# Column sums of a low-rank term in a fused FFN kernel: one fp32 selection matmul against two fp32r passes, and its place in the first block of a half

## The chip, the cores and the metric

The kernel runs on one core of one Trainium2 chip. The metric is the device time of one execution in microseconds, as the median of several. The arithmetic is fp32 throughout: TensorE takes fp32 operands either directly or as fp32r pairs (a rounded part and the remainder), which this kernel prepares on ScalarE (the rounded part) and GpSimd or VectorE (the remainder).

## The reference

2048 tokens of width 1024 go through two residual blocks with LayerNorm. The first is a gated FFN (2752 wide) in which the smaller half of each token's gate values is set to zero; the second is a gated FFN whose weights repeat four times and carry low-rank terms of rank 2. The change touches only the low-rank term of the second block's down projection.

```python
x = _layernorm(x + sparse_gated_ffn(x, w_gate, w_up, w_down))

def _qlora_linear(x, wq, A, B):
    w = jnp.tile(wq, (1, 4))
    return x @ w.T + (x @ A.T @ B.T) * 0.5
gate = jax.nn.silu(_qlora_linear(x, w1q, a1, b1))
up   = _qlora_linear(x, w3q, a3, b3)
x = _layernorm(x + _qlora_linear(gate * up, w2q, a2, b2))
```

With h = gate * up (2752 values a token), the down projection needs h folded four times (688 values) against w2q, and the two sums of h against the rows of a2, which are then multiplied by b2.

## The kernel before

The tokens are worked on in NB = 4 blocks of TB = 512, each of NT = 4 tiles of 128 tokens. The first FFN is `gate`, `up` and `down` for blocks 0 to 3 and takes the first 1436 us. The second FFN then runs in two halves h = 0 and 1; half h takes the blocks 2h and 2h + 1. A half is PAIRS = 11 pairs of steps for each of its two blocks (`pair(h, p, bb)`), and then `down_2(2h)` and `down_2(2h + 1)`, the down projections. Each engine has its own instruction stream written out by hand in this order, and the streams meet at semaphores only. Nothing is reordered by a scheduler.

**The sums of h.** In each pair VectorE multiplies gate and up (`h2`), adds them to the folded h (`fold`), and adds h times a column of a2 to `acc[:, bb, r, :]` for r = 0, 1 (four operations of 512 columns, line 1485). `acc` then holds, for 128 partitions, partial sums that still have to be summed over the partitions. After the last pair of a block VectorE raises `acc_ready` (`sums_done`).

**The selection, `low_rank_h(b)` on TensorE.** Two fp32 matmuls with `sel` (128 x 98, all zero but one column with 0.5) as the stationary operand sum `acc` over the partitions into rows 96 and 97 of PSUM bank 4, and raise `t2_done`. ScalarE's `high_t2(b)` (line 957) rounds the two rows into the last chunk of `hqh`; VectorE's `low_rank_h(b)` (line 1500) writes the remainder into `hql` and raises `t2_ready`. The last chunk (c = CQ - 1 = 5, 98 rows) of the down projection then carries the low-rank term with it.

**The down projection, `down_2(b)` on TensorE.** `product(t, n, c)` is three matmuls for token tile t, half n of the columns and chunk c. `all_but_last(t, n)` is the five chunks c = 0 to 4, so 15 matmuls. The results of tile t stand in banks 2(t % 2) + n. The order before is: tile 0 but for its last chunks, `low_rank_h(b)`, in block 0 the twelve transposes `turn_folded(2, k)`, then tile (1, 0) but for its last chunk, then a wait for `t2_ready`, the last chunks of (0, 0), (0, 1) and (1, 0), then (1, 1), and then tiles 2 and 3. Before tile t >= 2 it waits in `bank_waits(t)` until VectorE has taken tile t - 2 out of the same banks (`e_evac`, raised by `take_out`, line 1511).

**VectorE and ScalarE behind the selection.** VectorE's `second(0)` begins with `low_rank_h(0)`; behind it stand, in this order, `low_xf(2, 0)` and `(2, 1)` (line 1419, which wait for ScalarE's `high_xf`), `low_rank_x(2)`, two tiles of `norm_sums`, and only then `take_out(0, 0)`. ScalarE's `second(0)` begins with `high_t2(0)` and goes on to `high_xf(2, 0)` and `(2, 1)` (line 950). In blocks 2 and 3 `take_out` follows `low_rank_h` at once. GpSimd makes the remainders of the folded h (`low_q`, line 734) and of the weights (`low_13`, line 659). Ahead of the second FFN VectorE prepares its constants, `sel` among them (`fill`, line 1375, and line 1391), while GpSimd makes the last remainders of `w_down` and `w2`.

## Time and profile before

| | us |
|---|---|
| median of 3 runs | 1863.69 |
| lowest and highest | 1860.75, 1864.17 |
| profiled execution | 1862.13 |
| its span in the profile | 1860.2 |
| TensorE (PE) busy | 1840.7 |
| DVE, POOL, ACT busy | 1468.3, 957.5, 719.9 |

The profile gives the busy time of each engine, the chain of work that ended last, and the waits by engine and line. PE is TensorE, PEld its weight loads, DVE is VectorE, ACT is ScalarE, POOL is GpSimd. Times in rows are microseconds from the start of the span. A matmul of 512 columns is recorded with 0.39 us while the next one starts 0.23 us after it, so distances between starts are what a stream of matmuls costs.

### The profile page before, as it was taken

How to read it: one execution, taken by the hardware profiler on the slowest of the kernel's cores; microseconds unless marked ns; L12 is line 12 of the kernel's file. 1: busy time of each engine (PE TensorE's matmuls, PEld its weight loads, DVE VectorE, ACT ScalarE, POOL GpSimd, SP SyncE). 2: the span in 40 equal slices, each digit the busy share in tenths (PEclk: the TensorE clock that was granted, in tenths of full speed). 3: DMA queues.
4: the chain of work that ended last, by engine and by line, in shares of the span. 5: the costliest groups of instructions: out<-in, count | busy, mean ns of one | idle time of the engine just before them, and what ended most of it. 6: DMA issues, size and time to landing. Idle time of an engine off the chain costs nothing.

```text
span 1860.2 us, 23661 instructions
## 1 busy us (share of the span) xinstructions
PE 1840.7 (99%) x8584; PEld 1533.3 (82%) x8584; DVE 1468.3 (79%) x2077; ACT 719.9 (39%) x1177; POOL 957.5 (51%) x705
## 2 busy tenths in 40 slices
PE   9999999999999999999999999999999999999998
PEld 8898888978889789888888988888887777777776
DVE  2138899988988695898878768988588899889973
ACT  4346544474233434722343365233323232223312
POOL 5446697546655854465466545554568232023410
PEclk9999999999999999999999999999999999999999
DMA  4333248734377743334786334366953112312212
GB/s 147 93 101 97 86 147 236 204 98 142 97 232 227 226 129 104 113 128 131 236 256 195 93 107 142 98 212 193 278 179 141 35 46 101 135 62 77 102 46 91
DMA packets 123511, 258.65 MB, mean 139 GB/s; under 512 B 13860, under 2 KB 35876, under 8 KB 120168
## 3 DMA queue, kind: packets, MB, share of 16 engines
q1 hardware_dynamic: 118784, 240.34, 41.7%
q10 hardware_dynamic: 4608, 16.78, 2.2%
q8 instruction: 68, 1.11, 0.2%
q14 instruction: 51, 0.42, 0.1%
HBM read 215.65 MB, written 41.42 MB: 138 GB/s over the span
## 4 chain that ended last, share of the span: by engine, by line
PE 83%; POOL 5%; DVE 5%; ACT 4%; DMA 3%; issue 1%; SPq 0%; POOLq 0%; DVEq 0%; ACTq 0%
PE banks L1596 28%; PE banks L1597 27%; PE banks L1598 27%; POOL wl L659 3%; ACT junka L815 2%; DMA w_in_place<-in_wg 2%; DVE junkx L1083 1%; PE banks L1788 1%; POOL xTl L659 1%; ACT wh L766 1%; POOL w2l L659 1%; DMA w_in_place<-in_wd 0%; DVE qa L1125 0%; POOL w L688 0%; PE banks L1801 0%
## 5 line engine op out<-in xcount | busy, mean ns | idle before, releaser
L659 POOL TENSOR_TENSOR wl<-w_in_place,wh 128x512 fp32r<-128x512 f32 (+2 forms) x552 | 751.8, 1367 | 573.1 <-ACT wh L766 571.9
L766 ACT CAST wh<-w_in_place 128x512 fp32r<-128x512 f32 (+2 forms) x560 | 329.0, 589 | 724.2 <-DMA w_in_place<-in_wg 281.2
L1596 PE MATMUL banks<-wh,xTh 128*128 128x512 f32 (+2 forms) x1536 | 565.0, 368 | 5.4 <-POOL wl L659 5.3
L1598 PE MATMUL banks<-wh,xTl 128*128 128x512 f32 (+2 forms) x1536 | 563.2, 367 | 0.0
L1597 PE MATMUL banks<-wl,xTh 128*128 128x512 f32 (+2 forms) x1536 | 563.1, 367 | 0.0
L1596 PEld LDWEIGHTS banks<-wh,xTh 128*128 128x128 f32 x1536 | 288.3, 188 | 51.4 <-POOL wl L659 9.6
L1598 PEld LDWEIGHTS banks<-wh,xTl 128*128 128x128 f32 x1536 | 288.3, 188 | 40.1
L1597 PEld LDWEIGHTS banks<-wl,xTh 128*128 128x128 f32 x1536 | 288.3, 188 | 39.6
L1596 PE MATMUL banks<-wh,hTh 128*128 128x512 f32 x672 | 263.2, 392 | 2.2 <-POOL wl L659 2.1
L1598 PE MATMUL banks<-wh,hTl 128*128 128x512 f32 x672 | 262.2, 390 | 0.0
L1597 PE MATMUL banks<-wl,hTh 128*128 128x512 f32 x672 | 262.2, 390 | 0.0
L815 ACT ACTIVATE junka<-v,negt 128x1376 int8<-128x1376 f32 x96 | 138.3, 1441 | 79.4 <-DVE negt L1093 79.4
L1329 DVE TENSOR_TENSOR hTl<-landed,hTh 128x512 fp32r<-128x512 f32 (+1 forms) x96 | 105.2, 1126 | 73.7 <-ACT hTh L831 73.4
L1596 PEld LDWEIGHTS banks<-wh,hTh 128*128 128x128 f32 x672 | 126.6, 188 | 31.9 <-POOL wl L659 5.5
L1099 DVE TENSOR_SCALAR_CACHE_REDUCE junkd<-v,tc 128x2752 int8<-128x2752 f32 x48 | 147.6, 3076 | 0.9
L1598 PEld LDWEIGHTS banks<-wh,hTl 128*128 128x128 f32 x672 | 126.6, 188 | 26.3
L1597 PEld LDWEIGHTS banks<-wl,hTh 128*128 128x128 f32 x672 | 126.5, 188 | 25.9
L1485 DVE SCALAR_TENSOR_TENSOR acc<-h,a2raw,acc 128x512 f32<-128x512 f32 (+1 forms) x168 | 144.3, 900 | 1.5
L1596 PE MATMUL banks<-xsh,w13h 128*128 128x512 f32 (+1 forms) x352 | 142.5, 405 | 2.4 <-DVE y L1511 1.4
L1597 PE MATMUL banks<-xsl,w13h 128*128 128x512 f32 (+1 forms) x352 | 137.6, 391 | 0.0
L1598 PE MATMUL banks<-xsh,w13l 128*128 128x512 f32 (+1 forms) x352 | 137.3, 390 | 0.0
L659 POOL TENSOR_TENSOR w13l<-w_in_place,w13h 128x512 fp32r<-128x512 f32 x44 | 65.2, 1500 | 88.5 <-ACT w13h L945 88.4
(151 smaller groups left out, 2194.9 us busy)
## 6 DMA issues: line engine op xcount, KB each, us to landing
w_in_place<-in_wd SPq DMA_DIRECT2D x176, 256.0 KB, 2.7
w_in_place<-in_wg SPq DMA_DIRECT2D x128, 256.0 KB, 3.0
w_in_place<-in_wu SPq DMA_DIRECT2D x128, 256.0 KB, 2.7
turning<-squares SPq DMA_DIRECT2D x16, 1024.0 KB, 5.1
landed<-turning SPq DMA_DIRECT2D x64, 256.0 KB, 3.9
w_in_place<-in_w SPq DMA_DIRECT2D x54, 256.0 KB, 2.9
x_in_place<-in_xT SPq DMA_DIRECT2D x32, 256.0 KB, 5.2
y<-in_xtok SPq DMA_DIRECT2D x4, 2048.0 KB, 8.5
```

The lines of the kernel that those rows point to most:

```text
L659: nc.gpsimd.tensor_tensor(lo, landed, hi.bitcast(F32), ALU.subtract).then_inc(done, 1)
L766: nc.scalar.copy(hi, piece).then_inc(hi_done, 1)
L815: ins = nc.scalar.activation(junka[:, :], v[:, t, h * (I // 2):(h + 1) * (I // 2)], ACT.Sign, bias=negt[:, t:t + 1], accum_out=ssum[:, t - ...
L1083: step(V.scalar_tensor_tensor(out=junkx[:, :], in0=x[:, :], scalar=1.0, in1=v[:, R * w + r, I - H:I], op0=ALU.mult, op1=ALU.mult, accum_ou ...
L1099: step(V.tensor_scalar(junkd[:, :], v[:, t, :], tc[:, 0, t:t + 1], None, ALU.is_lt, ALU.add, accum_out=tc[:, 1, t:t + 1]))
L1329: V.tensor_tensor(h_part(hTl, j, g), h_part(landed, j, g), h_part(hTh, j, g).bitcast(F32), ALU.subtract).then_inc(t_lo, 1)
L1485: step(V.scalar_tensor_tensor(out=part, in0=h2[0:rows, i, :], scalar=w, in1=part, op0=ALU.mult, op1=ALU.add))
L1596: nc.tensor.matmul(dst, ah, bh, start=start, stop=False)
L1597: nc.tensor.matmul(dst, ah, bl, start=False, stop=False)
L1598: return nc.tensor.matmul(dst, al, bh, start=False, stop=stop)
L1788: nc.tensor.matmul(banks[4 * (s % 2) + 2 * w + i][0:rows, :], b13[p0:p0 + 3 * R, mm], lx[p0:p0 + 3 * R, bb, :], start=False, stop=True).th ...
```

## The change

The sums `acc` of a block are split like every other operand: ScalarE rounds them into `acch` (`high_sums(b)`, one cast of 128 x 1024, raising `acc_hi`), GpSimd writes the remainder over `acc`, under the name `accl` (`low_sums(b)`, one subtraction of 128 x 1024, raising `acc_lo`), and TensorE sums both over the partitions with `selr`, a copy of `sel` of the type fp32r. There is one `acch` for all blocks, so `high_sums(b)` waits for the selection of block b - 1 (`t2_done`). In the first block of a half (0 and 2) the selection moves from behind tile 0 to behind tile (1, 0), and the last chunks of tiles (0, 0), (0, 1) and (1, 0) move behind the first five of (1, 1). In blocks 1 and 3 the places stay. VectorE has one more copy, from `sel` to `selr`, in its preparation.

```diff
@@ GpSimd
+            def low_sums(b):
+                pool.wait_ge(acc_hi, b + 1)
+                nc.gpsimd.tensor_tensor(accl[:, b % 2, :, :], acc[:, b % 2, :, :], acch[:, :, :].bitcast(F32), ALU.subtract)\
+                    .then_inc(acc_lo, 1)
...
+                low_sums(2 * h)
                 low_q(h, CQ - 1, 1)
+                low_sums(2 * h + 1)
@@ ScalarE
+                high_sums(2 * h)
                 high_q(h, CQ - 1, 1)
+            def high_sums(b):
+                act.wait_ge(acc_ready, b + 1)
+                if b:
+                    act.wait_ge(t2_done, b)
+                nc.scalar.copy(acch[:, :, :], acc[:, b % 2, :, :]).then_inc(acc_hi, 1)
...
                 if b != 1:
                     high_t2(b)
+                if b % 2 == 0:
+                    high_sums(b + 1)
@@ VectorE
             for r in range(R):
-                V.memset(sel[:, r, T2 + r:T2 + r + 1], LORA).then_inc(sel_ready, 1)
+                fill(sel[:, r, T2 + r:T2 + r + 1], LORA)
+            V.tensor_copy(selr[:, :, :], sel[:, :, :]).then_inc(sel_ready, 1)
@@ TensorE
-                pe.wait_ge(acc_ready, b + 1)
+                pe.wait_ge(acc_lo, b + 1)
...
                 for r in range(R):
-                    ins = nc.tensor.matmul(banks[4][0:LR, :], sel[:, r, :], acc[:, b % 2, r, :], start=r == 0, stop=r == R - 1)
+                    nc.tensor.matmul(banks[4][0:LR, :], selr[:, r, :], acch[:, r, :], start=r == 0, stop=False)
+                    ins = nc.tensor.matmul(banks[4][0:LR, :], selr[:, r, :], accl[:, b % 2, r, :], start=False, stop=r == R - 1)
...
-                low_rank_h(b)
+                if b % 2:
+                    low_rank_h(b)
                 if b == 0:
                     for k in range(KQ + 1):
                         turn_folded(2, k)
                 bank_waits(1)
                 all_but_last(1, 0)
+                if b % 2 == 0:
+                    low_rank_h(b)
+                all_but_last(1, 1)
                 pe.wait_ge(ql_done, FOLDS * h + 2 * (CQ - 1) + bb + 1)
                 pe.wait_ge(t2_ready, b + 1)
                 pe.sem_inc(passed_pe, 1)
                 product(0, 0, CQ - 1)
                 product(0, 1, CQ - 1)
                 product(1, 0, CQ - 1)
-                all_but_last(1, 1)
                 product(1, 1, CQ - 1)
```

TensorE's stream in block 0, before: from the last matmul of tile (0, 1) to the first of tile (1, 0). `ident` with `xa` or `rep` are the transposes `turn_folded(2, k)`.

```order
L1598 MATMUL banks<-w2h,hq0l 128x512
L1801 MATMUL banks<-acc,sel 98x512 [waits acc_ready,s_done]
L1801 MATMUL banks<-acc,sel 98x512
L1730 MATMUL banks<-ident,xa 128x128 [waits h_done,xf_in]
L1730 MATMUL banks<-ident,xa 128x128 x3
L1730 MATMUL banks<-ident,xa 128x128 [waits h_done,xf_in]
L1730 MATMUL banks<-ident,xa 128x128 x3
L1730 MATMUL banks<-ident,rep_121 128x128 [waits h_done,rep_ready]
L1730 MATMUL banks<-ident,rep_121 128x128 x3
L1596 MATMUL banks<-w2h,hq0h 128x512 [waits h_done]
```

The same stream after, further on: the end of tile (1, 0) and the start of tile (1, 1).

```order
L1620 MATMUL banks<-w2h,hq0h 128x512
L1621 MATMUL banks<-w2l,hq0h 128x512
L1622 MATMUL banks<-w2h,hq0l 128x512
L1825 MATMUL banks<-acch,selr 98x512 [waits acc_lo,s_done]
L1826 MATMUL banks<-accl,selr 98x512
L1825 MATMUL banks<-acch,selr 98x512
L1826 MATMUL banks<-accl,selr 98x512
L1620 MATMUL banks<-w2h,hq0h 128x512
L1621 MATMUL banks<-w2l,hq0h 128x512
```

The selection now stands behind the twelve transposes and the 15 matmuls of tile (1, 0), has four matmuls for two, and waits for GpSimd in place of VectorE.

ScalarE's stream at the end of half 0, before:

```order
L971 CAST hq0h<-fold_115 96x512 [waits f_done]
L971 CAST hq1h<-fold_116 96x512 [waits f_done]
L957 CAST hq0h<-banks 2x512 [waits t2_done]
L950 CAST xsh<-banks 128x512 [waits xf_turned] x2
L852 ACTIVATE y<-y,nbias,rstd 128x1024 [waits nb_ready]
```

and after:

```order
L984 CAST hq0h<-fold_117 96x512 [waits f_done]
L1021 CAST acch<-acc 128x1024 [waits acc_ready]
L984 CAST hq1h<-fold_118 96x512 [waits f_done]
L970 CAST hq0h<-banks 2x512 [waits t2_done]
L1021 CAST acch<-acc 128x1024 [waits t2_done,acc_ready]
L963 CAST xsh<-banks 128x512 [waits xf_turned] x2
L865 ACTIVATE y<-y,nbias,rstd 128x1024 [waits nb_ready]
```

One cast of the sums stands ahead of the last `hq1h`, and the other between `high_t2(0)` and the two `xsh` casts.

## Rows read from the trace of the kernel before

**Rows 1.** The page: busy time of TensorE, share of the span, instructions.

```profile
PE 1840.7 (99%) x8584; PEld 1533.3 (82%) x8584; DVE 1468.3 (79%) x2077; ACT 719.9 (39%) x1177; POOL 957.5 (51%) x705
```

**Rows 2.** TensorE's waits in the whole run: us in total, times, longest.

```profile
PE banks L1596 <- POOL wl L659: 7.3, 13, 1.8
PE banks L1596 <- DVE y L1511: 1.4, 1, 1.4
```

**Rows 3.** Timeline of TensorE in block 0: start, us, line, operation, [idle before].

```profile
1581.79 1.88 PE L1801 MATMUL banks<-acc,sel 128*98 128x512 f32 x4
1583.51 1.04 PE L1730 MATMUL banks<-ident,xa 128*128 128x128 f32 x8
...
1584.74 0.47 PE L1596 MATMUL banks<-w2h,hq0h 128*128 128x512 f32 x1
...
1588.25 0.40 PE L1596 MATMUL banks<-w2h,hq0h 98*128 98x512 f32 x1
...
1594.44 0.39 PE L1596 MATMUL banks<-w2h,hq0h 128*128 128x512 f32 x1
```

**Rows 4.** Timeline of ScalarE in block 0: the two rows, then the folded x.

```profile
1583.71 0.58 ACT L957 CAST hq0h<-banks 2x512 fp32r<-2x512 f32 x1 [1.83 <-PE banks L1801]
1584.31 1.07 ACT L950 CAST xsh<-banks 128x512 fp32r<-128x512 f32 x2
```

**Rows 5.** Timeline of VectorE in block 0, from the last sums to the first tile out.

```profile
1575.05 3.88 DVE L1485 SCALAR_TENSOR_TENSOR acc<-h,a2raw,acc 96x512 f32<-96x512 f32 x4
...
1581.14 3.74 DVE L1485 SCALAR_TENSOR_TENSOR acc<-h,a2raw,acc 96x512 f32<-96x512 f32 x4
...
1585.85 1.29 DVE L1419 TENSOR_TENSOR xsl<-banks,xsh 128x512 fp32r<-128x512 f32 x2
...
1592.39 1.27 DVE L1511 TENSOR_TENSOR ya<-banks,ya 128x512 f32<-128x512 f32 x2
```

**Rows 6.** Timelines of GpSimd and VectorE where their operations overlap.

```profile
1581.95 1.71 POOL L734 TENSOR_TENSOR hq1l<-fold,hq1h 96x512 fp32r<-96x512 f32 x1 [3.57 <-ACT hq1h L971]
...
1582.58 1.64 DVE L1485 SCALAR_TENSOR_TENSOR acc<-h,a2raw,acc 96x512 f32<-96x512 f32 x1
```

**Rows 7.** Groups by form: the nearest rows to the added cast and subtraction.

```profile
L990 ACT ACTIVATE sg<-banks 128x1024 f32<-128x1024 f32 x40 | 41.1, 1028 | 150.5 <-PE banks L1788 134.9 <-DVE h L1465 9.1 <-issue 6.5
L734 POOL TENSOR_TENSOR hq0l<-fold,hq0h 128x512 fp32r<-128x512 f32 x10 | 14.6, 1464 | 77.9 <-ACT hq0h L971 77.9
```

**Rows 8.** Stretches: length, busy (x) of PE, PEld, DVE, ACT, POOL, then PEclk.

```profile
1429.00:1431.00 2.00, 1.75 (x5) 1.40 (x6) 2.00 (x4) 0.00 (x0) 2.00 (x3) 0.64 0.00 0
1431.00:1433.00 2.00, 2.00 (x6) 1.57 (x5) 2.00 (x4) 0.00 (x0) 1.92 (x2) 0.51 0.00 0
1433.00:1435.00 2.00, 2.00 (x10) 1.65 (x9) 2.00 (x4) 0.00 (x0) 0.00 (x0) 1.00 0.00 0
...
1651.00:1653.00 2.00, 1.96 (x9) 1.65 (x10) 1.82 (x4) 0.00 (x0) 0.00 (x0) 1.00 0.00 0
```

**Rows 9.** Timelines of VectorE and TensorE in block 1 and at the halves' border.

```profile
1621.71 0.70 DVE L1500 TENSOR_TENSOR hq1l<-banks,hq1h 2x512 fp32r<-2x512 f32 x1
...
1622.80 0.40 PE L1596 MATMUL banks<-w2h,hq1h 98*128 98x512 f32 x1
...
1651.04 0.47 PE L1596 MATMUL banks<-xsh,w13h 128*128 128x512 f32 x1 [1.42 <-DVE y L1511]
```

**Rows 10.** Timeline of VectorE between the two FFNs, behind the memsets of `sel`.

```profile
1405.51 0.91 DVE L1375 MEMSET rep<- 128x1024 f32 x1 [0.16 <-issue]
1406.46 1.18 DVE L1398 COPY rep<-dots 128x16 f32<-128x16 f32 x1
...
1438.42 2.48 DVE L1419 TENSOR_TENSOR xsl<-banks,xsh 128x512 fp32r<-128x512 f32 x4 [0.57 <-ACT xsh L950]
```

**Rows 11.** Timelines of TensorE and VectorE in block 2.

```profile
1795.05 0.40 PE L1596 MATMUL banks<-w2h,hq0h 98*128 98x512 f32 x1
...
1796.02 1.31 DVE L1511 TENSOR_TENSOR ya<-banks,ya 128x512 f32<-128x512 f32 x2 [2.09 <-PE banks L1598]
```

More of the change, by code:

```diff
@@ L297, in program @@
         rep = put("rep", [P, 2, NT, P], F32)
+        acch = put("acch", [P, R, TB], F32R)
         assert over["at"] <= at["hTh"]
@@ L320, in program @@
         assert over["at"] <= at["sgn"]
+        accl = sb("accl", [P, 2, R, TB], F32R, 4, offset=at["acc"])
         hqh, hql = (hq0h, hq1h), (hq0l, hq1l)
@@ L342, in program @@
         sel = put("sel", [P, R, LR], F32)
+        selr = put("selr", [P, R, LR], F32R)
+        assert over["at"] <= at["scr"] + 4 * H
         assert over["at"] <= at["mags"]
@@ L385, in program @@
         rep_ready, xf_turned, xs0_hi, xs0_ready = sem("rep_ready"), sem("xf_turned"), sem("xs0_hi"), sem("xs0_ready")
+        acc_hi, acc_lo = sem("acc_hi"), sem("acc_lo")
         acc_ready, t2_done, t2_hi, t2_ready = sem("acc_ready"), sem("t2_done"), sem("t2_hi"), sem("t2_ready")
@@ L1857, in _ @@
             pe.wait_ge(b_ready, 2)
-            pe.wait_ge(sel_ready, R)
+            pe.wait_ge(sel_ready, 1)
             pe.wait_ge(w2_lo, NW2)
```

## The prediction, made before the changed kernel ran

> **What bounds the kernel now.** I read the busy times first: TensorE is busy for 1840.7 of 1860.2 us [rows 1], so a microsecond saved on it is a microsecond saved, unless a wait takes its place. TensorE's list of waits comes next: in the whole second FFN there is one, 1.42 us for VectorE's take-out of a tile at the border of the halves; the 7.3 us for GpSimd lie in the first FFN, which is not touched [rows 2]. Everything else in the second FFN is on time, so the question is by how much. For that the timelines of the four engines around the selection are laid side by side [rows 3 to 6]. In them VectorE never pauses for over 0.6 us from 1585 to 1622 (its rows there are too many to show): whatever comes late there stays late until block 1. And its first tile is out at 1592.39 + 1.27 = 1593.66 [rows 5], while TensorE wants those banks at 1594.44 [rows 3]: 0.8 us in hand. That is the thinnest margin near the change.
>
> **The selection itself.** Its two fp32 matmuls hold TensorE from 1581.79 to 1583.51, 1.72 us [rows 3]. Four fp32r matmuls of the same 98 by 512 shape cost what the chunks with 98 rows cost: in block 0, 12 of them and 15 others run from 1588.25 to 1594.44, 6.19 us for 27, so 0.23 us each [rows 3]. Four are 0.92 us. Saved: 0.80 us a block, 3.2 us in all. TensorE has these on its path, so this is the whole possible gain.
>
> **The two new steps ahead of it, block 0.** The sums of block 0 are there at 1575.05 + 3.88 = 1578.9 [rows 5]. The cast of 128 x 1024 was never made; ScalarE's operation of that size out of PSUM takes 1.03 us [rows 7], two casts of 512 in a row 1.07 [rows 4]. I take 1.03, done at 1580.1. The subtraction of 128 x 1024 is twice the 1.46 us of a 512 one [rows 7], at most 2.9 us, so `acc_lo` comes by 1583.1. TensorE now passes the transposes (1.23 us) and tile (1, 0) (3.51 us) first, so it asks at 1581.79 + 1.23 + 3.51 = 1586.5 [rows 3]. No wait, with 3.4 us in hand.
>
> **What the subtraction does to VectorE.** Where GpSimd subtracts from 1581.95 to 1583.66, VectorE's operation started at 1582.58 takes 1.64 us; the other three of its four took (3.74 - 1.64) / 3 = 0.70 each [rows 5, 6]: one of the two stands still until the other is through. The Trainium skill, page "SBUF — State Buffer", section "Who interferes with whom", says that a VectorE instruction with two SBUF inputs and a GpSimd instruction that reads SBUF exclude each other for a whole instruction; the row agrees. The fold and sums of block 1 lie beside the new subtraction and can lose up to its whole length, so they end not at 1584.9 [rows 5] but by 1587.3 to 1587.8. VectorE's next step waits for the selection anyway, until 1588.2 (below). So this costs nothing, by 0.4 us at least.
>
> **The later place, block 0: the price.** The selection is off TensorE at 1586.53 + 0.92 = 1587.45. ScalarE began `high_t2` 0.20 us after the stream's end (1583.71 against 1583.51) [rows 3, 4]: now 1587.65, done 1588.25. Then comes the second new cast, for block 1, 1.03 us, until 1589.3; only then the first `xsh` cast, 0.6 us, which VectorE waits for. VectorE's `xsl` starts at 1589.9 where it started at 1585.85 [rows 5]: 4.1 us late. Everything behind it in VectorE's queue is as late: `low_rank_x`, the norm sums, and `take_out(0, 0)`, which ends at 1593.66 + 4.07 = 1597.7. TensorE, 0.80 us earlier than before, wants the banks at 1593.64 and gets them at about 1597.9. A wait of 4.25 us takes the place of none. Of the 4.1 us, 3.0 come from the later place of the selection and 1.0 from the cast for block 1 in ScalarE's queue.
>
> **The clock behind that wait.** TensorE's longest wait, 1.8 us for GpSimd [rows 2], ends just inside the first stretch of rows 8. There the granted clock was 0.64 and in the next two microseconds 0.51, the 1.2 GHz level, and then full again. Lost: 1.75 x 0.36 + 2.00 x 0.49 = 1.6 us. After the 1.42 us wait at the border the clock held (the last row of the group) [rows 8, 9]. A wait of 4.25 us is well above both, so I expect a drop. Its cost lies between 0 (the low level falls into the wait itself) and 1.6 us; I take 1.1, since part of it should fall into the wait.
>
> **Block 1.** TensorE saves another 0.80, so its own path puts it at -0.8 + 4.25 + 1.1 - 0.8 = 3.8 us late at the last chunks. But those also need `t2_ready` from VectorE. Before, VectorE wrote it from 1621.71 to 1622.41 and TensorE used it at 1622.80 [rows 9], 0.24 us in hand when the 0.15 us of a semaphore is taken off. VectorE is 4.1 us late there, so TensorE is at least 4.1 - 0.24 = 3.9 us late. The clock's share thus hardly matters: 3.9 holds for any of its values up to 1.2, and at 1.6 it is 4.3. In block 1 VectorE works for what TensorE delivers and the other way round until the border [rows 9], so the 3.9 stays. The subtraction for block 1 starts at 1589.3 and ends by 1592.3; the selection of block 1 comes near 1621. Nothing waits for it.
>
> **Blocks 2 and 3.** The same later place costs nothing here: `take_out(2, 0)` follows the selection's remainder at once. It began 0.97 us after TensorE's first last-chunk matmul, at 1796.02 against 1795.05, and took 1.31 us [rows 11], so both halves are out 2.3 us after it. TensorE now does the four last chunks in a row, 12 matmuls, 2.76 us, before it wants those banks: 0.3 us in hand with the semaphore. The two blocks keep their 1.6 us.
>
> **VectorE's extra copy between the FFNs.** Its tiny copies there took 1.18 us [rows 10], since each stands until a GpSimd operation is through. The new cast of 128 x 196 does the same, but the next copy would have waited for the same place: the memset between them, 0.91 us, fits into GpSimd's next 1.25. The Trainium skill's section named above says that casts can take the shared port; without that rule the cast would cost 0.1 us, with it some 0.25 of shift. Behind it VectorE had 0.57 us in hand before `xsl` at 1438.42 [rows 10], but GpSimd shifts too. I take +0.2; the bounds are 0 and, if the memset misses the place and the queue shifts by 1.5 us, 1.5 - 0.6 = 0.9.
>
> **The sum.** 3.9 (late at the border) - 1.6 (blocks 2 and 3) + 0.2 = +2.5 us against the profiled execution's 1862.13 (span 1860.2), which lies 1.6 below the median of the three runs. The tail behind the last matmul is unchanged. On the median, 1863.69 + 2.5 = 1866.2. The extremes of the unknown costs are 3.6 - 1.6 + 0.0 = +2.0 and 4.3 - 1.6 + 0.9 = +3.6.
>
> **The rivals.**
> (a) The low clock outlasts the wait. A wait of more than twice 1.8 us could bring a low spell of twice the length behind it, 3.2 us lost. Then TensorE's own path decides: -1.6 + 4.25 + 3.2 = 5.9, the total is 5.9 - 1.6 + 0.2 = +4.5, so 1868.2, slower by 0.24%. It decides from a clock loss of 1.2 us on, and makes the change slower than what can be told apart from about 2.4 us on. For it: the 1.8 us wait shows that a drop happens. Against it: the spell ended there within four microseconds although TensorE worked at half speed. The Trainium skill, page "TensorE: Matmul & The Clock Gate", section "What's actually happening", calls the low clock the default that activity releases; by that the whole spell of 1.6 us would follow the wait and the sum be +2.9.
> (b) The gain arrives. If VectorE were not late at the first tile, the total is -3.2 + 0.2 = -3.0, so 1860.7, 0.16% faster. For it: TensorE had only one wait. Against it: it needs `xsl` no more than 0.0 us late (0.8 in hand, less the 0.8 saved), where three dependent steps put it at 4.1.
> (c) The subtraction of 1024 columns comes too late for the selection in block 0. It would need over 6 us where two of 512 take 2.9, and then adds its excess: at 8 us +1.5 more, 1867.7. Small.
> (d) The change does not do what it says: the fp32r matmuls of this shape cost more than 0.23 us. The last chunks with 98 rows speak against it [rows 3]. If they cost 0.43, nothing is saved and the total is +5.7.
>
> **How the numbers follow.** A difference of about 0.2%, 3.7 us, is what a measurement of this kernel can tell from no change. Forecast 0.68; (a) 0.13; (b) 0.12; (c) and (d) 0.03 together; 0.04 left open. Slower by over 0.2% gets (a), (c), (d) and the forecast's upper edge: 0.20. Faster by over 0.2% would take (b) and another gain beside it: 0.04. Within it: 0.76. The forecast's own range is 1865.7 to 1867.3; the runs before lie from 2.9 below to 0.5 above their median. With this scatter and most of (a) the range is 1863.0 to 1868.6.
>
> **What would show it.** TensorE's waits: a new one of about 4.2 us for VectorE's `ya` in block 0, near 1594. PEclk near half behind it, for two to four microseconds. VectorE's first `xsl` of block 0 near 1590, directly behind ScalarE's second cast of the sums. TensorE at the border at about 1655, with the 1.4 us wait still there. No TensorE wait for GpSimd's `accl`, and none in block 2. The selection at 0.23 us from matmul to matmul. The prediction is wrong if `take_out(0, 0)` ends before 1594, or if block 2 has a wait of its own.

## The result, and the profile after

The changed kernel's median is 1869.80 us (1865.31 to 1873.06) against 1861.76 (1858.79 to 1865.97) for the kernel before on the same chip: ratio 1.0041, interval 1.0030 to 1.0052. A second measurement gave 1868.88, ratio 1.0036 (1.0021 to 1.0050). The forecast was 1866.2 and "within 0.2%", with a range up to 1868.6. It came out slower by over 0.2% and above the range: 8.0 us where 2.5 were forecast. The profiled execution took 1869.9 us; its span is 1868.0.

The page of the changed kernel, busy times, against [rows 1]:

```profile
PE 1840.0 (98%) x8584; PEld 1536.1 (82%) x8584; DVE 1462.7 (78%) x2078; ACT 724.6 (39%) x1181; POOL 971.1 (52%) x709
```

Its TensorE waits, against [rows 2]:

```profile
PE banks L1620 <- POOL wl L664: 7.1, 11, 1.7
PE banks L1620 <- DVE ya L1535: 4.1, 1, 4.1
PE banks L1620 <- DVE y L1535: 3.3, 1, 3.3
PE banks L1620 <- DVE h L1489: 2.6, 2, 2.4
```

Three waits in the second FFN where there was one. `ya` was forecast. The border's `y` has grown from 1.4 to 3.3, and `h` is new. TensorE's timeline, against [rows 3] and [rows 9] (the selection, then where it resumes behind each wait):

```profile
1573.67 0.47 PE L1620 MATMUL banks<-w2h,hq0h 128*128 128x512 f32 x1 [2.42 <-DVE h L1489]
...
1586.94 0.40 PE L1825 MATMUL banks<-acch,selr 128*98 128x512 f32 x1
1587.17 0.39 PE L1826 MATMUL banks<-accl,selr 128*98 128x512 f32 x1
...
1598.32 0.47 PE L1620 MATMUL banks<-w2h,hq0h 128*128 128x512 f32 x1 [4.11 <-DVE ya L1535]
...
1657.75 0.76 PE L1620 MATMUL banks<-xsh,w13h 128*128 128x512 f32 x1 [3.33 <-DVE y L1535]
```

ScalarE and VectorE in block 0, against [rows 4] and [rows 5]:

```profile
1588.07 0.58 ACT L970 CAST hq0h<-banks 2x512 fp32r<-2x512 f32 x1 [5.39 <-PE banks L1826]
1588.67 1.05 ACT L1021 CAST acch<-acc 128x1024 fp32r<-128x1024 f32 x1
1589.74 1.08 ACT L963 CAST xsh<-banks 128x512 fp32r<-128x512 f32 x2
```

```profile
1590.37 1.29 DVE L1443 TENSOR_TENSOR xsl<-banks,xsh 128x512 fp32r<-128x512 f32 x2 [0.99 <-ACT xsh L963]
...
1596.90 1.27 DVE L1535 TENSOR_TENSOR ya<-banks,ya 128x512 f32<-128x512 f32 x2
```

The chain is the one forecast: remainder of the selection, a cast of 1.05 us in ScalarE's queue, `xsh`, `xsl`, and `take_out(0, 0)` done at 1598.17.

**A ruler for the second FFN.** Whole times of one kernel scatter by 7 us and more (1858.79 to 1865.97 above). In the two traced executions of each of the two kernels that scatter lies in the first FFN: from the first matmul with `xsh` to the end of the span, the kernel before took 420.0 us in both, and the changed kernel 431.9 in both. So I measure from that matmul (1440.22 before, 1436.09 after) and list how much later each kernel passes five places than the kernel before does (the first matmul of each `down_2`, the first matmul of half 1, the end of the span, which the page gives to 0.1 us). "pad" marks empty instructions and "again" a second execution, both explained below. Each line is one execution, while each median is of 7 to 12.

| kernel | down_2(0) | down_2(1) | half 1 | down_2(2) | end | median us, ratio to before |
|---|---|---|---|---|---|---|
| changed | 2.96 | 9.74 | 8.92 | 13.55 | 11.93 | 1869.80, 1.0041 |
| after_again | 3.10 | 11.12 | 10.30 | 13.52 | 11.96 | 1868.88, 1.0036 |
| before_again | 0.00 | 0.00 | 0.00 | 0.00 | 0.06 | 1858.03, one execution |
| odd_back | 2.98 | 9.69 | 9.32 | 9.33 | 7.76 | 1867.27, 1.0020 |
| order_only | 1.72 | 8.30 | 8.29 | 10.22 | 10.25 | 1871.91, 1.0039 |
| split_only | 0.33 | 4.33 | 3.98 | 3.98 | 4.32 | 1865.87, 1.0014 |
| norm_first | 2.92 | 5.10 | 4.29 | 8.93 | 7.32 | 1867.12, 1.0019 |
| all_three | 2.93 | 6.22 | 5.84 | 5.85 | 4.26 | 1861.91, 0.9994 |
| best2 | 2.94 | 3.42 | 4.27 | 4.25 | 2.66 | 1861.20, 0.9996 |
| cast_only | 2.94 | 4.34 | 4.35 | 4.34 | 4.40 | 1863.25, 0.9998 |
| before_pad10 | 0.02 | 0.02 | 0.02 | 0.08 | 0.15 | 1860.58, 0.9992 |
| before_pad34 | 0.37 | 0.31 | 0.32 | 0.33 | 0.34 | 1860.27, 0.9993 |
| after_pad34 | -0.02 | 5.73 | 4.92 | 9.60 | 8.01 | 1866.46, 1.0034 |
| odd_pad34 | 0.11 | 6.40 | 6.01 | 6.02 | 4.46 | 1863.54, 1.0008 |
| three_pad34 | 0.01 | 1.86 | 1.80 | 1.81 | 0.29 | 1859.66, 0.9995 |

The changed kernel's 11.93 us, read along its line: 2.96 for the pairs' end and the wait for `h`; 6.78 in block 0 (low clock behind that wait 1.6, selection -0.8, wait 4.1, low clock behind it 1.9); -0.82 in block 1, the selection's saving; 4.63 behind the border (1.91 more wait, 2.72 low clock); -1.62 in blocks 2 and 3. The second execution, `after_again`, has the same three waits and the same end, but it is 1.4 us later at `down_2(1)` and gets that back at the border: how much low clock follows a wait is another matter in each execution. So a difference of 1 to 2 us between two lines of the table can be this, and not the kernel, wherever a wait of over 1.5 us lies before it. The medians differ by 8.0 and 6.2 us in the two measurements, less than 11.93. Where the rest is stays open (sections 5 and 7).

### The profile page after: what moved, and what is told of

The parts are those of the page before. It is cut to its first block and busy times, and to the rows that moved or that the text cites. A ratio compares the mean times of both kernels' runs of the same rounds, so it can differ in the third digit from the quotient of the medians.

```text
span 1868.0 us, 23673 instructions
## 1 busy us (share of the span) xinstructions
PE 1840.0 (98%) x8584; PEld 1536.1 (82%) x8584; DVE 1462.7 (78%) x2078; ACT 724.6 (39%) x1181; POOL 971.1 (52%) x709
## 5 line engine op out<-in xcount | busy, mean ns | idle before, releaser
L1509 DVE SCALAR_TENSOR_TENSOR acc<-h,a2raw,acc 128x512 f32<-128x512 f32 (+1 forms) x168 | 151.6, 942 | 1.6
L1003 ACT ACTIVATE sg<-banks 128x1024 f32<-128x1024 f32 (+1 forms) x44 | 45.2, 1028 | 177.2 <-PE banks L1812 118.9
```

The lines of the kernel that those rows point to most:

```text
L1003: nc.scalar.activation(sg[0:rows, :, :], psum[0:rows, 4 * (s % 2):4 * (s % 2) + 2, :], ACT.Silu)\
L1509: step(V.scalar_tensor_tensor(out=part, in0=h2[0:rows, i, :], scalar=w, in1=part, op0=ALU.mult, op1=ALU.add))
```

## The experiments

Each was measured beside the kernel before on its chip; its line in the table is the reading, and short diffs are against the changed kernel unless said.

**1. The places in blocks 1 and 3.** The diff moves `all_but_last(1, 1)` ahead of the last chunks in every block, and the prediction had blocks 1 and 3 unchanged. `odd_back` puts those two back.

```diff
                 if b % 2 == 0:
                     low_rank_h(b)
-                all_but_last(1, 1)
+                    all_but_last(1, 1)
...
                 product(1, 0, CQ - 1)
+                if b % 2:
+                    all_but_last(1, 1)
                 product(1, 1, CQ - 1)
```

> The changed kernel, but in blocks 1 and 3 the first five chunks of tile (1, 1) stand behind the last chunks again, as before the change; blocks 0 and 2 keep the new order. Theory N (the new order of the chunks in block 1 lets VectorE's take-out of tile (1, 0 to 1) begin 3.5 us later, VectorE is dense from there to the border of the halves, and so TensorE waits 3.3 us there and then runs at half clock for a while, 2.7 us): the wait at the border is about 1.4 us again, no low clock behind it, and the time is 4 to 5 us below the changed kernel's, so +2.5 to +3.5 us against the kernel before. Rival R (all of the loss comes from the 4.1 us wait in block 0): no difference to the changed kernel, +7 to +8 us against before.

TensorE's waits in `odd_back`:

```profile
PE banks L1620 <- DVE ya L1535: 4.1, 1, 4.1
PE banks L1620 <- DVE h L1489: 2.7, 2, 2.4
...
PE banks L1620 <- DVE y L1535: 1.4, 1, 1.4
```

Up to the border TensorE is within 0.4 us of the changed kernel, the border has its old 1.4, and half 1 starts its work 4.2 us earlier (9.33 against 13.55). So the place in block 1 costs 4.2 us in this pair of executions: 1.9 of wait, which every kernel with this place shows, and low clock behind it, which varies (below). The median, 4.2 us above the kernel before, was expected at 2.5 to 3.5 above. VectorE's timeline of the changed kernel shows how, against [rows 9]:

```profile
1627.16 0.70 DVE L1524 TENSOR_TENSOR hq1l<-banks,hq1h 2x512 fp32r<-2x512 f32 x1
1631.98 1.31 DVE L1535 TENSOR_TENSOR y<-banks,y 128x512 f32<-128x512 f32 x2 [4.13 <-PE banks L1622]
...
1656.91 1.29 DVE L1535 TENSOR_TENSOR y<-banks,y 128x512 f32<-128x512 f32 x2 [0.22 <-DVE lx L1478]
```

Behind its remainder VectorE stands 4.13 us for the first tile, which is complete only at the last chunks, since the 15 matmuls of (1, 1) now lie ahead of them. In the kernel before it stood 1.36:

```profile
1623.77 1.31 DVE L1511 TENSOR_TENSOR y<-banks,y 128x512 f32<-128x512 f32 x2 [1.36 <-PE banks L1598]
```

By the ruler that tile is taken 12.3 us late (195.89 against 183.55), while TensorE itself is some 9 us late. VectorE's rows from there to the border have no idle time of over 0.3 us, so it arrives at the border's banks with the 2.8 us idled away still missing.

**2. The order alone, and the split alone.** `order_only` is the kernel before with the new places and its two fp32 matmuls; `split_only` has the casts, subtractions and fp32r matmuls in the old places. The diff is that of `split_only`; `order_only` makes the same moves the other way round in the kernel before.

```diff
-                if b % 2:
-                    low_rank_h(b)
+                low_rank_h(b)
                 if b == 0:
                     for k in range(KQ + 1):
                         turn_folded(2, k)
                 bank_waits(1)
                 all_but_last(1, 0)
-                if b % 2 == 0:
-                    low_rank_h(b)
-                all_but_last(1, 1)
...
                 product(1, 0, CQ - 1)
+                all_but_last(1, 1)
                 product(1, 1, CQ - 1)
```

> The kernel before with nothing but the new order on TensorE: selection behind tile (1, 0) in blocks 0 and 2, last chunks behind the first five of (1, 1) in all blocks; fp32 selection, no split. Theory N: block 0 waits about 3.2 us for the first tile (VectorE's xsl 3.9 us late) and loses some 1.6 to the clock, the border waits 3 to 4 us and loses 2.7 to the clock; nothing is saved on the selection: +8 to +10 us against before. Rival S (the added casts and subtractions are what costs): within 2 us of before.

> The changed kernel with TensorE's old order in all blocks: the fp32r split alone. Theory N: TensorE waits about 1 us for GpSimd's remainder in block 0 and in block 2; ScalarE's cast for block 1 waits for VectorE's sums (held up by the subtraction until some 2.2 us later) and the xsh casts stand behind it, so xsl is about 3 us late and the first tile makes TensorE wait about 2 us, with or without 1.6 us of low clock; the border as before the change. In all +0.5 to +3 us against before, 5 to 7 below the changed kernel. Rival S: the same as the changed kernel, +7 to +8.

TensorE's waits in `order_only`:

```profile
PE banks L1596 <- DVE y L1511: 3.3, 1, 3.3
PE banks L1596 <- DVE ya L1511: 3.1, 1, 3.1
...
PE banks L1596 <- DVE h L1465: 1.7, 1, 1.7
```

It waits 3.1 us for `ya` and 3.3 at the border, and saves nothing in blocks 2 and 3 (10.22 to 10.25): the later place alone makes both waits. `ya` is 1.0 shorter than in the changed kernel, the cast that stands ahead of `xsh` there. It also waits 1.7 us for `h`, before any of its moved instructions (section 5). `split_only` waits twice for the remainder, `ya` 1.7, the border at its old value:

```profile
PE banks L1825 <- POOL accl L739: 2.0, 2, 1.0
PE banks L1620 <- DVE ya L1535: 1.7, 1, 1.7
...
PE banks L1620 <- DVE y L1535: 1.4, 1, 1.4
```

So the old places would have cost 1.0 us of wait in each of blocks 0 and 2, and 1.7 for `ya` with low clock behind it (4.33 at `down_2(1)`); the later place trades that for 4.1 and the border. Neither half gives a gain.

**3. What stands ahead of the first tile on VectorE.** `norm_first` uses the time in which VectorE waits for the selection for two tiles' norm sums, which otherwise stand ahead of `take_out(0, 0)`.

```diff
+                if b == 0:
+                    norm_sums(NB - 1, lambda t: y[:, t, :], [0, 1])
                 low_rank_h(b)
...
                     low_rank_x(2)
-                    norm_sums(NB - 1, lambda t: y[:, t, :], [0, 1])
                     take_out(0, 0)
```

> The changed kernel; VectorE does the norm sums of two tiles of x1 of block 3 (3 us) ahead of the selection's remainder in block 0, where it idles otherwise. Theory N: the wait in block 0 shrinks from 4.1 to about 1.1 us, without low clock; the border still waits 3 to 4 us and loses the clock, since block 1's order is unchanged: 3 to 5 us below the changed kernel, +3 to +4.5 against before. Rival R: +0 to +2 against before, since all the loss was in block 0.

```profile
PE banks L1621 <- DVE y L1535: 3.3, 1, 3.3
PE banks L1621 <- DVE h L1489: 2.5, 1, 2.5
...
PE banks L1621 <- DVE ya L1535: 1.1, 1, 1.1
```

`ya` falls from 4.1 to 1.1 and down_2(1) comes 4.6 us earlier: 3.0 of wait and 1.6 of low clock. A wait of 1.1 us brings no low clock. It also shows that block 0's lateness isn't what made the border long: that stays at 3.3.

**4. Combined.** `all_three` has 1 and 3 and the cast for block 1 behind the `xsh` casts. `best2` has in addition the selection of blocks 0 and 2 behind two chunks of (1, 1), a third tile of norm sums ahead, `take_out(0, 0)` ahead of `low_rank_x`, and GpSimd's first remainder later.

> The changed kernel with three repairs: the old order of the last chunks in blocks 1 and 3 (as in odd_back), VectorE's norm sums of two tiles ahead of the selection's remainder in block 0 (as in norm_first), and ScalarE's cast of the sums for block 1 behind the two xsh casts. Theory N: the wait in block 0 shrinks to 0.5 us, since xsl no longer waits for ScalarE (norm_first had 1.15 with 0.53 of that); the border waits 1.4 to 3 us, since VectorE still starts its dense stretch some 2.3 us late behind GpSimd's subtraction; no low clock in block 0. In all -0.5 to +2 us against before. Rival T (the gains of norm_first and odd_back are one and the same and do not add): +3 to +4 us.

> As all_three, and made so that nothing holds up VectorE's last sums: in half 0 GpSimd subtracts the sums of block 0 only after VectorE has finished those of block 1; TensorE's selection in blocks 0 and 2 stands behind two more chunks, inside tile (1, 1); VectorE does the norm sums of three tiles ahead of the selection's remainder and takes the first tile out before low_rank_x. Theory N: VectorE's dense stretch begins 2.3 us earlier than in all_three, no wait over 0.5 us in block 0 and for the selection, the border waits 1.4 to 3 us; -3 to -1 us against before, 1 to 3 us below all_three. Rival L (the lock between GpSimd's subtraction and VectorE costs nothing that matters): the same as all_three.

`all_three` ends 4.26 behind before by the ruler and waits 1.9 for `ya`, where 0.5 was expected. Its VectorE starts `xsl` 0.5 us earlier than `norm_first`'s by the ruler, as planned, but its TensorE comes to the banks 1.3 us earlier: in this execution the clock held behind the wait for `h` (below), and fell behind the one for `ya`. `best2` has no `ya` wait and ends at 2.66, where 1 to 3 us ahead of before were expected; it waits 1.43 us for VectorE's remainder in block 1 (written from 1624.55 to 1625.25) instead. Both medians cannot be told from the kernel before. All of `all_three`'s 4.26 and more was there by down_2(1), and 2.93 of it already at down_2(0): the wait for `h`, where no edit of this change has run yet but VectorE's copy.

**5. Repeats of both kernels.**

> The kernel before, unchanged, for a second trace. The pairs of half 0 are the same work in every kernel here, but VectorE's product of the first block's last pair came too late for TensorE by 2.4 us in the changed kernel and was on time in the kernel before. Theory V (this wait varies from execution to execution with the arrival of the weights, and has nothing to do with the change): a wait of anything from 0 to 2.5 us at the start of block 0's down projection. Rival C (the change brings it): no wait.

> The changed kernel, unchanged. Theory V: the waits of 4.1 us in block 0 and 3.3 us at the border appear again to 0.1 us, the one ahead of block 0 with another length. The ratio to before is 1.003 to 1.005 again.

The second execution of the kernel before took 1858.03 us and started its second FFN at 1436.06 where the first started it at 1440.22; the second of the changed kernel started it at 1438.16. Both of the kernel before have no wait for `h`, both of the changed one have 2.42 us, where another length was expected for the second. The start of the second FFN thus belongs to the execution. That the wait belongs to the kernel is not shown by two executions of each, and `order_only` speaks against it: up to this wait its instructions are those of the kernel before, and it waits 1.68 us.

**6. Where the wait for `h` comes from.** By the ruler VectorE's pairs in both kernels run alike, to 0.1 us, up to 64 us behind the first matmul. There ScalarE casts two weight pieces. Its timeline in the kernel before, then in the changed one:

```profile
1504.09 0.62 ACT L945 CAST w13h<-w_in_place 128x512 fp32r<-128x512 f32 x1 [1.51 <-DMA w_in_place<-in_w]
1506.07 0.62 ACT L945 CAST w13h<-w_in_place 128x512 fp32r<-128x512 f32 x1 [1.35 <-DMA w_in_place<-in_w]
```

```profile
1501.84 1.25 ACT L958 CAST w13h<-w_in_place 128x512 fp32r<-128x512 f32 x2 [3.37 <-DMA w_in_place<-in_w]
```

63.87 and 65.85 behind the start of the pairs, against 65.75 for both: the first piece lands 1.9 us later. The DMA view shows what is in its way. One packet of code (the queue marked "instruction"; that it is TensorE's shows below, where instructions added to TensorE's stream move it) starts in the middle of the load, and some packets of the weights end late. Changed kernel: the stretch of the load, then the 2 us behind its main part:

```profile
q8 instruction: 1, 0.02, 0.4%
...
w_in_place<-in_w SPq DMA_DIRECT2D x2, 256.0 KB, 4.9
```

```profile
DMA packets 18, 0.03 MB, mean 16 GB/s; under 512 B 2, under 2 KB 2, under 8 KB 18
```

and the kernel before, the same two stretches:

```profile
w_in_place<-in_w SPq DMA_DIRECT2D x2, 256.0 KB, 3.7
```

```profile
DMA packets 9, 0.02 MB, mean 8 GB/s; under 512 B 1, under 2 KB 1, under 8 KB 9
```

The load is 288 packets over 16 engines, 9 for each piece on each. I read 18 packets late as both pieces behind the code, and 9 as the second alone; the view does not name the engine of a packet. The packets under 512 B, two against one, fit this: a piece of 256 KB is eight packets of 2 KB and a small one on each engine. It is a near thing: the code packet starts 63.33 and 63.34 us behind the first matmul in the two executions of the kernel before and 63.48 in `split_only` (9 late each), but 63.28 in `cast_only`, 63.21 and 62.69 in the changed kernel and 62.19 in `order_only` (18 late each). Two executions of one kernel differ by 0.5 us here, and 0.05 us separates a kernel with the wait from one without. GpSimd then makes both remainders in one go beside VectorE's sums. VectorE's timeline, before and changed:

```profile
1506.56 3.90 DVE L1485 SCALAR_TENSOR_TENSOR acc<-h,a2raw,acc 128x512 f32<-128x512 f32 x4
```

```profile
1502.33 4.80 DVE L1509 SCALAR_TENSOR_TENSOR acc<-h,a2raw,acc 128x512 f32<-128x512 f32 x4
```

and after that step it is 1.2 to 4.3 us later at each pair, and 3.1 at block 0's last (136.05 against 132.97 by the ruler). I read the first delay as VectorE standing for GpSimd; how it grows from pair to pair was not followed. To move the code transfer, empty instructions (a semaphore increment that nobody waits for) were put into TensorE's stream ahead of the second FFN, 10 or 34 of them:

```diff
                     for t in range(NT):
+                        if b == NB - 1 and 1 <= NT * (ND - d) - t - 4 <= 34:
+                            pe.sem_inc(passed_pe, 1)
                         if d < 2:
```

> The kernel before with 10 empty instructions (semaphore increments that nobody waits for) in TensorE's stream, spread over the last products of down(3), so that every later piece of TensorE's code begins about 10 instructions earlier in the program: 27 us between code transfers for 256 instructions, so 1.05 us. Theory K (a code transfer that falls ahead of the first of two weight pieces on one DMA engine makes VectorE's pairs late, and so the 2.4 us wait for h at the start of down_2(0) in the changed kernel): in the kernel before the transfer lies between the two pieces at 63.2 us behind the first pair's start; 1.05 us earlier it lies ahead of the first. ScalarE's cast of that piece comes at 65.7 behind the start of the pairs in place of 63.9, a wait of 1.5 to 2.5 us for h appears before down_2(0), with a low clock behind it, and the time is 2 to 4 us longer. Theory V (the wait comes from the arrival of the whole pair phase, or from the changed order itself): no wait for h, same time as before within 1 us.

> The kernel before with 34 such empty instructions. Theory K: the code transfer moves 3.6 us earlier and is through before the weight pieces start; no wait for h before down_2(0), the first piece's cast at 63.3 to 63.9 us behind the start of the pairs, time within 1.5 us of before. Empty instructions themselves cost nothing, since TensorE's sequencer has 0.23 us a matmul. Rival: they cost 0.05 us each, 1.7 us in all, and then before_pad10 costs 0.5.

> The changed kernel with 34 such empty instructions in down(3). Theory K: the wait of 2.42 us for h before down_2(0) and the 1.6 us of low clock behind it go; the waits of 4.1 us for ya and 3.3 us at the border stay; 3 to 4 us faster than the changed kernel, ratio to before 1.0015 to 1.0025. Theory V: the wait for h stays at 1.7 to 2.5 us and the ratio at 1.0036 to 1.0041.

> all_three (places of blocks 1 and 3 undone, two norm sums ahead of the remainder of the selection, the second cast of the sums behind the folded x) with the 34 empty instructions. Theory K: without the wait for h (2.46 us and its clock) 3 to 4 us faster than all_three: ratio to before 0.997 to 0.9985. Theory V: as all_three, 0.9994.

In `after_pad34` the transfer comes 56.4 us behind the start of the pairs, the load lands in 2.7 us with nothing late, and the wait for `h` is gone from TensorE's list:

```profile
w_in_place<-in_w SPq DMA_DIRECT2D x2, 256.0 KB, 2.7
```

```profile
PE banks L1620 <- DVE ya L1535: 4.1, 1, 4.1
PE banks L1620 <- DVE y L1535: 3.3, 1, 3.3
```

down_2(0) is at -0.02 in place of 2.96, and the second FFN is 3.9 us shorter (427.99 against 431.91). `three_pad34` is 4.0 shorter than `all_three` and level with before by the ruler (0.29). That this packet's place makes the wait for `h` is thus shown: all three kernels that were padded out of it lose it. The medians show less of it. `after_pad34` came out at 1.0034 (1.0021 to 1.0047), 4.7 us above before where 6.2 and 8.0 were measured without the pad, and above the 1.0015 to 1.0025 expected; `three_pad34` is at 0.9995 like `all_three` at 0.9994, where 0.997 to 0.9985 was expected. Only `odd_pad34` (0.5 us above before, below) against `odd_back` (4.2 above) shows it in full. `before_pad10` missed its expectation: the transfer moved by 4.4 us and not by 1.05, to 58.9, so it too left the load, and 10 instructions cost nothing. My scale of 0.105 us an instruction doesn't hold; what sets the transfer's time is open. The direction expected of it (a harmed kernel before) was thus not tried by it; `cast_only` and `order_only` are such kernels.

**7. VectorE's copy alone, and the prediction's own sum.** `cast_only` is the kernel before with the copy to `selr`, which nothing reads (diff against before):

```diff
+        selr = put("selr", [P, R, LR], F32R)
...
-                V.memset(sel[:, r, T2 + r:T2 + r + 1], LORA).then_inc(sel_ready, 1)
+                fill(sel[:, r, T2 + r:T2 + r + 1], LORA)
+            V.tensor_copy(selr[:, :, :], sel[:, :, :]).then_inc(sel_ready, 1)
```

> The kernel before with VectorE's added copy from sel to selr alone; nothing reads selr, and the selection is the fp32 one. The second FFN, from its first matmul with xsh to the end of the span, should be 420.0 us long as before, without a wait for h. The stated price of the copy was +0.2 us, bounds 0 and 0.9: ratio 0.9995 to 1.0005. Rival: the copy makes the part ahead of the second FFN shorter, since kernels that have it give medians that lie up to 4 us below what their second FFN alone would make them: then the median is 2 to 4 us below before, ratio 0.998 to 0.999.

> odd_back (the changed kernel with the old places of the last chunks in blocks 1 and 3) with the 34 empty instructions in down(3): what the prediction had summed, a late block 0 and nothing else. The second FFN should be 420.0 + 2.5 to 4.0 us long, with a wait of 4.1 us for ya, 1.4 at the border and none for h; the median 0 to 4 us above before, ratio 1.000 to 1.002. If the low clock behind the wait for ya costs 1.1 us, as forecast, it is 2.5; each microsecond more of it is at most one more.

`cast_only` has the wait for `h`, 18 packets late in the same place, and a second FFN of 424.4 us:

```profile
PE banks L1599 <- DVE h L1468: 2.6, 2, 2.4
```

Its median is nevertheless that of before (0.9998, 0.9986 to 1.0010). Either its first part is some 4 us shorter on average, or the wait for `h` is missing in many executions of it, or present in many of the kernel before. The traces do not decide: its second FFN starts at 1438.02, between the two executions of before (1436.06 and 1440.22), and no kernel but the two main ones was traced twice. The same 4 to 6 us stand open between ruler and median in the changed kernel. For the first reading speaks that the median's excess over before is 1.4 to 1.9 us below the ruler's in the three kernels without the copy (`order_only` and the two padded ones) and 1.5 to 5.7 below it in those with it.

`odd_pad34` has neither `h` nor the longer border, which is the case that the prediction summed: +4.46 by the ruler, where the prediction had +2.3 for it (3.9 - 1.6). Its `ya` wait is 4.12 us. The low clock behind it costs 3.0, read off its line (6.40 - 0.11, less 4.12, plus the saving of 0.8). Its ratio, 1.0008 (0.9996 to 1.0020), is what the prediction said of the whole change: within 0.2%.

## Why the prediction was wrong

**Right.** The selection at 0.23 us a matmul and 0.8 saved a block: rows 1586.94 and 1587.17, and -0.82 and -1.62 in the table. The cast (1.05, 1.03 forecast). The chain of three steps and its price: `xsl` behind ScalarE's second cast, and a wait of 4.11 us where 4.25 was forecast; the split into 3.0 for the place and 1.0 for the cast is what `order_only` shows (3.14). No wait for `accl`, and none in block 2. The subtraction took 2.39 us (at most 2.9 forecast), and VectorE stood for it, without a cost, as said:

```profile
1579.08 2.39 POOL L739 TENSOR_TENSOR accl<-acc,acch 128x1024 fp32r<-128x1024 f32 x1 [2.53 <-ACT acch L1021]
```

```profile
1579.36 2.66 DVE L1494 TENSOR_TENSOR fold<-h 96x512 f32<-96x512 f32 x1
```

The fold took 0.69 us in other pairs. What the prediction cited from the Trainium skill, page "SBUF — State Buffer", section "Who interferes with whom", agrees with this row. One bound in the sum has no source: the 3.6 us at the lower end follows from nothing ahead of it, where block 1 gave 3.9 as the least.

**The step that failed: block 1.** "In block 1 VectorE works for what TensorE delivers and the other way round until the border, so the 3.9 stays", and with it "TensorE at the border at about 1655, with the 1.4 us wait still there". The text on the change, too, says "In blocks 1 and 3 the places stay". That holds for `low_rank_h` alone; the diff takes `all_but_last(1, 1)` ahead of the last chunks in all four blocks, and the order of instructions was printed for block 0 only. It costs 1.9 us more wait at the border and 2.7 of low clock behind it; `odd_back` gives 4.2 of the 4.6 back. The 1.9 are there in all five executions with this place. The low clock is not: it took 2.7 here, 1.3 in `after_again` and nothing in `order_only`, behind the same wait of 3.3 us. In the medians, undoing the place took away 3.8 and 2.0 us (`odd_back` against the changed kernel's two) and 4.2 (`odd_pad34` against `after_pad34`). In blocks 2 and 3 the same move is free, as argued for block 2.

**A term mis-sized: the clock.** Forecast 1.1 behind the 4.25 us wait, at most 1.6. Behind the 4.1 us wait it was 1.9 in the changed kernel, 2.4 in `after_pad34` and 3.0 in `odd_pad34`; behind the border's 3.3 it was 2.7, but see above. The stretches (the columns are those of [rows 8]), changed kernel at the border:

```profile
1656.00:1658.00 2.00, 0.25 (x1) 0.28 (x2) 1.78 (x3) 0.00 (x0) 0.00 (x0) 0.77 0.00 0
1658.00:1660.00 2.00, 2.00 (x5) 1.53 (x6) 1.69 (x4) 0.00 (x0) 0.00 (x0) 0.50 0.00 0
1660.00:1662.00 2.00, 2.00 (x6) 1.60 (x5) 0.83 (x2) 0.00 (x0) 1.70 (x2) 0.50 0.01 4
1662.00:1664.00 2.00, 2.00 (x8) 0.81 (x8) 0.57 (x1) 0.00 (x0) 1.78 (x2) 0.52 0.00 0
```

and `odd_pad34` behind its `ya` wait:

```profile
1593.00:1595.00 2.00, 1.28 (x3) 1.12 (x4) 1.85 (x4) 0.00 (x0) 0.00 (x0) 0.50 0.00 0
1595.00:1597.00 2.00, 2.00 (x6) 1.52 (x6) 1.68 (x6) 0.00 (x0) 0.00 (x0) 0.50 0.01 4
1597.00:1599.00 2.00, 2.00 (x7) 1.52 (x6) 1.80 (x5) 0.70 (x1) 1.01 (x1) 0.50 0.00 0
1599.00:1601.00 2.00, 2.00 (x9) 1.64 (x8) 1.85 (x4) 1.60 (x2) 0.00 (x0) 0.85 0.31 127
```

The 1.2 GHz level lasts for about six microseconds of work there, against less than four behind the 1.8 us wait. "Part of it should fall into the wait" came out in some executions: in the changed kernel the clock stayed at 1.00 until the end of the `ya` wait, but in `after_pad34` it fell some 2 us before that end, and the spell still cost 2.4:

```profile
1592.00:1594.00 2.00, 0.00 (x0) 0.00 (x0) 1.85 (x5) 0.00 (x0) 0.00 (x0) 0.59 0.00 0
1594.00:1596.00 2.00, 1.41 (x3) 1.17 (x4) 1.85 (x5) 0.00 (x0) 0.00 (x0) 0.50 0.00 0
```

And it need not fall at all. `order_only` behind its border wait of 3.35 us, and `all_three` behind its 2.46 us for `h`:

```profile
1662.00:1664.00 2.00, 2.00 (x9) 1.65 (x10) 1.82 (x4) 0.00 (x0) 0.00 (x0) 1.00 0.00 0
```

```profile
1575.00:1577.00 2.00, 1.89 (x8) 1.61 (x9) 1.97 (x4) 1.43 (x2) 0.49 (x1) 1.00 0.99 418
```

The prediction gave the Trainium skill's view of this (page "TensorE: Matmul & The Clock Gate", section "What's actually happening": low clock as the default that activity releases) as +0.4 on the sum. Behind the changed kernel's `ya` wait the spell followed the wait whole, as the prediction read that view, and cost 1.9; behind that of `after_pad34` it did not. Rival (a) had the right mechanism, a spell of twice the length behind the wait: its 3.2 us and +4.5 are what `odd_pad34` shows (3.0 and 4.46). Its chance was too small, but the changed kernel's own execution had only 1.9, so that this term alone does not account for the miss.

**Not foreseen: the code transfer.** The wait for `h` and its clock, 3.9 us by the ruler, don't come from an order or a cost in the diff. `cast_only`, with one added instruction on VectorE, has it, and so has `order_only` without any. The prediction's term for that copy (+0.2, at most 0.9) stands against 4.4 us in the second FFN of `cast_only`'s traced execution and 0 in its median.

**Together.** +2.3 forecast for the second FFN; +2.2 for the low clock behind `ya` and small terms (`odd_pad34`, 4.46); +3.6 for the place in block 1 (`after_pad34`, 8.01); +3.9 for `h` (11.93). These are differences between single executions, each with 1 to 2 us of low clock that may or may not fall. The median's 8.0 and 6.2 are 4 to 6 us less, and why is open. With `three_pad34` the whole idea comes out level with the kernel before: ratio 0.9995 (0.9986 to 1.0004), while the kernel before with the same pad has 0.9993. No version tried is faster than before by more than the measurement can tell.

## What to carry to other kernels

Print the order of every block that a diff touches, not only the one that the change names: a step that moves ahead of a completion delays whoever waits for that completion, and an engine that is dense from there to the next border delivers the delay in full. Price a new wait of TensorE with the low clock behind it, from 0 to 3 us here for waits of 1.7 to 3.4 and 1.7 to 3 for waits of 4.1. And measure a change from a mark inside the kernel: the ruler's totals here agreed to 0.1 us where whole times scattered by 7, and it separated causes that the medians mixed. But trace each kernel more than once: two executions of the changed kernel were 1.4 us apart in between, and what one trace shows need not be what the median is made of.

## What the runs showed of the hardware

- A single packet of TensorE's code, in the middle of a load of two 256 KB pieces, made the first piece 1.9 us late, and the traced second FFN 3.9 us longer. Ten empty instructions in TensorE's stream moved the packet 4.4 us, out of the load. With 18 weight packets late, TensorE waited 1.7 to 2.5 us in all seven kernels concerned, with 9 late 0 and 0.26, and with none in the load 0 to 0.29.
- Low clock behind a wait in the second FFN: none behind any of 1.0 to 1.4 us. Behind 1.7 to 1.9 it came in three of four cases, behind 2.4 to 2.5 in six of seven, behind the single 3.1 once, behind 3.3 in four of five, behind 4.1 in all five. Where it came it cost 1.3 to 3.1 us, in no order with the length of the wait.
- A VectorE fold of 96 x 512 took 2.66 us beside a GpSimd subtraction of 128 x 1024 (2.39 us) and 0.69 in other pairs. A weight piece that GpSimd got 1.9 us later was followed by VectorE being 1.2 to 4.3 us late in every later pair of that half.
